# Four layers of cross-attention and feed-forward on one core: the first gated products fed from TensorE, setup reordered

## The chip, the core and the metric

One core of one Trainium2 chip. The metric is the device time of one execution in microseconds, from the kernel's runs; the profile is of one execution. All tensors are float32. In the names below, PE is TensorE, DVE is VectorE, ACT is ScalarE, POOL is GpSimd and SP is the queue that issues the DMAs.

## The reference, cut to what matters

Eight sequences (B=8) of 128 rows and 128 columns pass through four layers, each a cross-attention and a feed-forward block, each with a layer norm in front and a residual around it:

```python
x = x + L0_xattn(ctx, ctx, layernorm(x))
x = x + L0_ffn(layernorm(x))
x = x + L1_xattn(layernorm(x), ctx, ctx, masks)
x = x + L1_ffn(layernorm(x))
x = x + L2_xattn(layernorm(x), ctx, mask)
x = x + L2_ffn(layernorm(x))
x = x + L3_xattn(layernorm(x), ctx, ctx, bias)
x = x + L3_ffn(layernorm(x))
```

The block that matters most here is `L0_ffn`, an attention whose values and outputs are mixtures of experts, with 8 heads and 8 experts a head:

```python
gate_v, gate_o = sel_gate(x, sel_v_w), sel_gate(x, sel_o_w)   # two of eight experts, sigmoid, normalised, dense [S, 8, 8]
v = einsum('bshep,bshe->bhsp', einsum('bsd,hedp->bshep', x, v_w), gate_v)
att = softmax(einsum('bhqp,bhkp->bhqk', q, k) * SCALE)
ctx = einsum('bhqk,bhkp->bqhp', att, v)
out = einsum('bshep,hepd->bsd', ctx[..., None, :] * gate_o[..., None], o_w)
```

## The kernel before

The eight sequences are taken as four pairs of two (a lane each). The work is cut into four streams. *Early* (`early_pair`, letter p in the order table) does layer 0's attention of a pair and everything of `L0_ffn` up to the gates and the transposed probabilities. *Front* (`front_pair`, letter f) does the expert products of `L0_ffn`. *Back* (`back_lane`, letters 0 and 1 for the two lanes) does layers 1 to 3 of a pair. `late_setup`, at the head of stream 0, folds and centres weights once. Each engine has its own list of steps of each stream, and `ORDER`, a table written out by hand for each engine, says which stream takes its next step (`weave`, L353). Every engine works through that list in order; semaphores connect them.

A pair's expert products are 32 tiles of eight products: 16 for the values (head n // 2, lane n % 2), four mixing steps, and 16 for the outputs. A tile needs the gated rows, `gated` (128 x 1024): the transposed activations times the gate of each of eight experts, where the gate of a row stands in every partition. To bring it there, VectorE transposes the gates in blocks of 32 (`turn_gates`, L1542), SP stores them to a DRAM tensor in four pieces so that rows come out as columns (L404), and loads eight rows back, broadcast to all partitions, 512 KB a tile (`spread_gates`, L382); VectorE then multiplies in place (`gated_tile`, L1576, an instruction recorded at L1433). There are six slots for `gated` and four for the experts' weights, 512 KB each and one for two tiles; a load waits until the products that used its slot are done. All DMAs go through SP, in the order of its table.

The core of the front on TensorE (`expert_products`):

```python
pe.wait_ge(f_gated_ready, n + 1)
for e in range(E):
    ins = mm(to, gated[n % G_SLOTS][:, S * e:S * e + S],
             weights[j % W_SLOTS][:, D * e:D * e + D], first and e == 0, last and e == E - 1)
```

A float32 product shows in the trace as two matmul instructions (passes), a transposition as one; a tile is thus 16 passes. PSUM has eight banks: `e_bank` for expert products, `p_bank` for the early stream, and three for each lane. For pair 0, lane 0's early units use `e_bank` (`unit_bank`, L350), so pair 0's first expert product waits until the early stream is through.

`late_setup` on TensorE (L633) makes the folded q-k products, the total for layer 1's ternary weights, two value folds, the bias and mean of `proj`, and then the centred weights of layers 1 to 3, in six banks; ScalarE copies each result out (L1074), VectorE computes thresholds, the ternary weights, the length sums and scalings (L1617). The back's lanes wait on all engines for the last of these (`CENTRED`), GpSimd's masks of lane 0 and 1 among them (`masks`, L1336). `first_loads` (L416) issues all weights at the start. ScalarE's Gelu in layer 1's feed-forward (L1177) and in layer 2's (L1216) needs another activation table than the exponentials; a table load stands in the trace wherever the function changes. After the last front, TensorE does SPARE = 24 groups of three transpositions of the identity in its order's gaps (L627).

Of the kernel before, what the change touches and what calls it, by code (L numbers as in the profile page):

```python
# [11 lines left out]
E = 8  # L12
# [9 lines left out]
SPARE = 24  # L22
TILES = 4 * H0F
# [21 lines left out]
    "PE": "pppppp000p0pppp0ppp0000ppppppfpffpfpffpffpffpffpffffpfpfpfpfpfffffpffffpffpfffffp00p01p10pffff010pf0"  # L45
          "ff000fp00f00pffp0f0p10ff1ff00pf001f0110fp0f0p0110100000100101f10p0f11p0f11f10001f01f1p1ff1f11p1111f1"
          "0p0110f10f10011p010ff1pff0p001p10p10pfff1f0101ffff1p10ffffp1f11p0fpf1f01p010f10fp10f010f11pf00p1f111"
          "1f10p11f110011f101010ff0101pf0p01f11p0f00011000p00010110f011p1001f1101fp0f0010ff1001p10100f11f100110"
          "f0fp11f1f10p101ff00ff00f010000pf0010ff00f010110f01100101f1110f1100f101f1011001ff10ff101010110100010f"
          "ff100011f1f10111010f10f01101f11f1010fff11101010101ff1fffffff1f1ffff101011110010101011001101001001101"  # L50
          "00f0ffff10110011101000000000101101000011101000100101011f111100101101fffff",
    "Activation": "pppppp0p0pp000ppp00pppppppppp000pfppfpfpfpfpfpfp0fppppppp000p01p01fp00000000ppf010p001p0f0111f0f001f"
                  "0p11fp000110p000011f10p1111p01100011001pp11111p0010p00001100011pp011p00p1ppp11110f01111pf000fp1111p0"
                  "0p1f1000f11f01f000pf1p1110011p11111110111000p111p0010pp10p00001101p0011p0p11000000111000p10111001000"
                  "0p111111f011p10100f000p0001010000f01p110001110011f00111f110f10f11f1010011101101010000000110101001110"
                  "1111000001111111110101011111011100101110001101010011100101000110011100100000100001010000011001011011"
                  "011111011100011",
    "DVE": "pppppp0p0pppppp00pppppppppppp0ppffpppfppffffpffpffppffffppppfffffppfpppfpffpppffppfppfpffpppffppffff"
           "ffffp01f0000000f0fffp11f10fpf0001ffp1p11fp1000f00f000f100ppp0000p10000p0p1111ffffff1001101f01ff0p011"
           "ppp10111110pp1p11ffppff0ppp1100000010p11101f0ff0ffff1pppp0fffff000p1ff11ff0000p111111fff1p011pp11p11"  # L60
           "1110ff01pfppppff110fff01101010ff110f01p1f100p0ppp111100f0010000p000pp11p1111fpppp000000f01f01111ppp1"
           "1ppf10ffff0f00000001f01110111110ff11ff1ff0000ff0000111fff0011f100011000011000111ff001110000f1f11f000"
           "010ffff0011100000111111f10ffff111101111000f00f0010011111111f10ff101011111101001000101111001010010101"
           "010110001111000000110000011100000001011111011000000001111111110101",
    "Pool": "ppppfff1110000110100000p00011p11000000011110111110010001111fff1001p00000111p111000111110101011001001"
            "100000111f1ff010001100001000111010111010100011010000111111101f01ff0101111100001111000101010000010011"
            "1011",
    "SP": "ppffpffffffffpffffffffffffffffffffpffffpfffffffffffffpffffffffffffff0f1ffpffpfffffffffffffffffffpfff"
          "ffffffff10ffffff1fpffff0ffffpfffffffffffff0ffff1f1fffff0fffffff0011fff",
}  # L70


def width(members):
    return sum(n for _, n in members)


def build(nc, x_in, ctx_in, q_mask, k_mask, pair_mask, packs, experts, gates_of, out):
    with ExitStack() as stack:
# [3 lines left out]
        def sem(name):  # L82
            return stack.enter_context(nc.semaphore(name))
# [1911 lines left out]
```

## Time and profile before

| what | value |
|---|---|
| median of three runs | 682.85 us (681.27 to 683.88) |
| the profiled execution's own time | 681.64 us |
| its span, first to last instruction | 680.0 us |
| TensorE busy | 631.2 us (93%), 5480 passes |
| VectorE busy | 515.6 us (76%) |
| ScalarE busy | 372.9 us (55%) |
| GpSimd busy | 209.4 us (31%) |
| moved by DMA | 113.98 MB, mean 168 GB/s |

The span is what the trace covers; the own time is what the runs measure, 1.64 us more. Matmuls are pipelined and their ends are modelled, so a busy TensorE is not one at its peak: the number of passes in a stretch says more. Durations in the rows are microseconds unless marked ns; L464 is the helper that records every product, L980 ScalarE's copies, L1429 to L1436 VectorE's helpers, so tiles tell more than lines. Idle time in brackets names what ended it.

### The profile page before, as it was taken

Reading aid. Unit: us, or ns where it says so; the run is one execution under the profiler, and the core shown is the slowest. Engines: PE = TensorE matmul, PEld = TensorE weight load, DVE = VectorE, ACT = ScalarE, POOL = GpSimd, SP = SyncE. Lnnn points to the kernel's source line nnn. Section 1 sums busy time; section 2 is a strip of 40 time slices with the busy share of each in tenths; the row PEclk is TensorE's granted clock in tenths of the full one; section 3 lists DMA queues with packets and bytes.
Section 4 is the critical chain, followed back from the end, with each engine's and each line's share of the span. In section 5 each row is a group of like instructions: output and inputs, shape, how many; then the busy total and the mean of one; then the engine's idle time right before and its main releaser. Section 6 shows DMA issues by size and latency. Waiting matters only on the chain.

```text
span 680.0 us, 14643 instructions
## 1 busy us (share of the span) xinstructions
PE 631.2 (93%) x5480; PEld 576.7 (85%) x5480; DVE 515.6 (76%) x1419; ACT 372.9 (55%) x1257; POOL 209.4 (31%) x252
## 2 busy tenths in 40 slices
PE   5979999989999999998999999989999989899888
PEld 4868999868889999998789998977889989668877
DVE  1987678657678888895797889888368967657766
ACT  2361231346563667434845867356775563787594
POOL 0000000773440233231612625054243350642150
PEclk9899999979999999999999999999999999999999
DMA  8969969857704372987245316575416520000000
GB/s 321 402 237 298 364 239 334 303 180 271 239 1 159 99 265 72 340 267 269 77 155 192 109 32 191 189 239 173 156 28 229 171 79 1 6 1 1 1 2 12
DMA packets 37654, 113.98 MB, mean 168 GB/s; under 512 B 9040, under 2 KB 11728, under 8 KB 37072
## 3 DMA queue, kind: packets, MB, share of 16 engines
q1 hardware_dynamic: 37584, 113.06, 48.8%
q8 instruction: 43, 0.70, 0.4%
q14 instruction: 27, 0.22, 0.1%
HBM read 111.99 MB, written 1.05 MB: 166 GB/s over the span
## 4 chain that ended last, share of the span: by engine, by line
PE 53%; DVE 24%; ACT 11%; DMA 5%; POOL 5%; issue 3%; SPq 1%; DVEq 0%; POOLq 0%; ACTq 0%
PE bank L464 23%; PE e_bank L464 20%; DVE gated L1433 7%; ACT wide_b L1125 6%; PE p_bank L464 4%; DMA gated<-gates_of 4%; DVE wide_b L1436 2%; DVE max_neg L1721 2%; PE bank L721 2%; ACT wide_a L980 1%; DVE x L1436 1%; DVE f_route L1433 1%; DVE f_xn L1430 1%; ACT L1177 1%; PE bank L710 1%
## 5 line engine op out<-in xcount | busy, mean ns | idle before, releaser
L464 PE MATMUL e_bank<-weights,gated 128*128 128x128 f32 x2048 | 244.4, 277 | 2.4 <-DVE gated L1433 1.3
L464 PEld LDWEIGHTS e_bank<-weights,gated 128*128 128x128 f32 x2048 | 236.7, 193 | 6.3 <-issue 2.5
L1125 ACT ACTIVATE wide_b<-wide_b,max_neg 128x120 f32<-128x120 f32 x272 | 103.6, 388 | 22.7 <-DVE max_neg L1721 17.7
L1331 POOL TENSOR_TENSOR wide_b<-wide_b,row_inv 128x480 f32<-128x480 f32 x64 | 69.2, 1087 | 111.4 <-DVE row_inv L1726 111.1
L1433 DVE TENSOR_TENSOR gated<-gated,f_xnT 128x1024 f32<-128x1024 f32 x64 | 82.3, 1313 | 10.6 <-DMA gated<-gates_of 9.8
L1323 POOL TENSOR_TENSOR rstd<-var_eps,w_const 128x1 f32<-128x1 f32 (+1 forms) x48 | 35.2, 736 | 168.7 <-DVE var_eps L1429 168.5
L1433 DVE TENSOR_TENSOR gated<-gated,f_v 128x1024 f32<-128x1024 f32 x64 | 76.9, 1232 | 10.6 <-ACT f_v L980 5.5
L980 ACT ACTIVATE wide_a<-bank 120x512 f32<-120x512 f32 (+5 forms) x111 | 57.7, 540 | 43.9 <-PE bank L721 21.8
L1125 ACT ACTIVATION_READ_ACCUMULATOR wide_b<-wide_b,max_neg 128x1 f32 x272 | 52.6, 193 | 0.0
L1721 DVE TENSOR_REDUCE max_neg<-wide_b 128x4 f32<-128x480 f32 x64 | 41.8, 653 | 2.2
L721 PE MATMUL bank<-w_const,wide_b 128*120 128x128 f32 x256 | 37.4, 275 | 6.0 <-POOL wide_b L1331 5.9
L980 ACT ACTIVATE f_v<-e_bank 128x512 f32<-128x512 f32 x32 | 19.2, 600 | 37.6 <-PE e_bank L464 37.3
L721 PEld LDWEIGHTS bank<-w_const,wide_b 128*120 128x120 f32 x256 | 28.6, 138 | 12.1 <-issue 9.2
L1216 ACT ACTIVATE wide_a<-bank,w_L2f 128x128 f32<-128x128 f32 x128 | 34.8, 400 | 4.7 <-PE bank L464 4.7
L980 ACT ACTIVATE xnT<-bank 128x128 f32<-128x128 f32 x48 | 13.4, 282 | 37.8 <-PE bank L710 37.7
L464 PE MATMUL bank<-xnT,w_L2f 128*128 128x128 f32 x256 | 31.9, 278 | 0.0
L464 PE MATMUL bank<-w_L2f,wide_a 128*128 128x128 f32 x256 | 31.8, 275 | 0.0
L464 PEld LDWEIGHTS bank<-w_L2f,wide_a 128*128 128x128 f32 x256 | 30.2, 192 | 0.6 <-issue 0.5
L464 PEld LDWEIGHTS bank<-xnT,w_L2f 128*128 128x128 f32 x256 | 30.0, 192 | 0.1
L980 ACT ACTIVATE wide_b<-bank 128x480 f32<-128x480 f32 (+2 forms) x40 | 20.7, 523 | 15.1 <-PE bank L464 15.1
L1726 DVE RECIPROCAL row_inv<-row_sum 128x4 f32<-128x4 f32 x64 | 10.5, 170 | 23.8 <-ACT wide_b L1125 23.6
L1030 ACT ACTIVATE f_b<-p_bank,f_max_neg 128x128 f32<-128x128 f32 x56 | 19.7, 366 | 13.7 <-DVE f_max_neg L1495 13.7
(264 smaller groups left out, 1221.6 us busy)
## 6 DMA issues: line engine op xcount, KB each, us to landing
gated<-gates_of SPq DMA_DIRECT2D x128, 512.0 KB, 5.7
weights<-in_experts SPq DMA_DIRECT2D x64, 512.0 KB, 6.2
w_L2f<-in_L2f SPq DMA_DIRECT2D x1, 2124.0 KB, 14.6
w_L3x<-in_L3x SPq DMA_DIRECT2D x1, 2108.0 KB, 19.5
w_L3f<-in_L3f SPq DMA_DIRECT2D x1, 1128.0 KB, 21.6
wide_b<-in_raw0f SPq DMA_DIRECT2D x1, 1024.0 KB, 7.8
w_L1f<-in_L1f SPq DMA_DIRECT2D x1, 516.0 KB, 10.6
x_next<-in_x SPq DMA_DIRECT2D x4, 128.0 KB, 5.1
```

Source lines behind the costliest of these rows:

```text
L464: return nc.tensor.matmul(o, lhsT, rhs, start=first, stop=last)
L721: last = nc.tensor.transpose(bank[lane][(1, 2, 0, 1)[i]][0:K, 128 * c:128 * c + 128], wide_b[lane][:, K * h:K * h + K], ident)
L980: return nc.scalar.activation(o, i, ACT.Identity, bias=bias, scale=scale)
L1030: last = nc.scalar.activation(f_b[lane][:, 128 * h:128 * h + 128], unit_bank(pair, lane)[:, 128 * c:128 * c + 128], ACT.Exp, bias=f_max_ne ...
L1125: last = nc.scalar.activation(p, p, ACT.Exp, bias=max_neg[lane][:, h:h + 1], accum_out=row_sum[lane][:, h:h + 1])
L1216: last = nc.scalar.activation(wide_a[lane][:, at:at + 128], bank[lane][(1, 0, 2, 1)[i]][:, 128 * c:128 * c + 128], ACT.Gelu, bias=part["L2 ...
L1323: nc.gpsimd.tensor_tensor(rstd[lane][:, cols], var_eps[lane][:, cols], part["const", "minus_half"][:, 0:cols.stop - cols.start], ALU.pow)\
L1331: nc.gpsimd.tensor_tensor(p3, p3, row_inv[lane][:, 4 * i:4 * i + 4].unsqueeze(2).broadcast_to([128, 4, K]), ALU.mult).then_inc(probs_norme ...
L1433: return nc.vector.tensor_tensor(o, a, c, op)
L1436: return nc.vector.scalar_tensor_tensor(o, a, scalar, c, op0, op1)
L1721: nc.vector.tensor_reduce(max_neg[lane][:, 4 * i:4 * i + 4], s3, AX.X, ALU.max, negate=True)\
L1726: nc.vector.reciprocal(row_inv[lane][:, 4 * i:4 * i + 4], row_sum[lane][:, 4 * i:4 * i + 4])\
```

## The change

Eight edits go together:

1. **Spread on TensorE.** The first TURNED = 8 tiles of pair 0 don't go through DRAM. TensorE transposes a column of `f_gate`, repeated 128 times, so that the gate stands in all partitions: four such transpositions fill a bank with four experts' gates (`turn_first_gates`), in the three banks of lane 1 by turns. VectorE multiplies from PSUM in halves of 128 x 512 into one of two buffers in `wide_b[0]`. The spread loads of these tiles go.
2. **Early units.** For pair 0, lane 0's early units use `bank[0][2]` instead of `e_bank`, and the first expert product no longer waits for the transposed probabilities.
3. **Setup in two banks.** From the value folds on, setup's products use `bank[0][0]` and `bank[0][1]` by turns (the second value fold `bank[1][2]`), each waiting for ScalarE's copy of the bank's content before. The last fold waits for `ROUTED_IN`.
4. **Loads.** The packs L2x, L3x and L3f go ahead of the experts' first weights, which get a semaphore for each slot; layer 1's context goes behind the lengths.
5. **Zero products.** VectorE clears a tile `idle`; TensorE multiplies it with itself 7 times at the start, and 3, 3, 1, 5, 1 and 4 times behind the steps of pair 0's first attention, into `e_bank`, which no one reads.
6. **Early Gelu loads.** Right after the transposed x of layer 1's feed-forward is copied, ScalarE does a Gelu of one column of ones into `gelu_once`, eight times in all.
7. **memset.** Clearing `gate` goes from `late_setup` to the start.
8. **Order.** `ORDER` is new for all five engines. At the start, VectorE's length sums and the scaling of `proj` come behind pair 0's first gates, TensorE's mean of `proj` and all centring behind the first expert products, the last folds and GpSimd's masks of lane 0 ahead of the end of pair 0's front. SP issues the store of the second gates ahead of tile 8's load.

```diff
+TURNED = 8
...
+        first_gated = [wide_b[0][:, 1024 * i:1024 * i + 1024] for i in range(2)]
+        first_spread = [bank[1][i] for i in range(3)]
...
         def unit_bank(pair, lane):
-            return e_bank if pair == 0 and lane == 0 else p_bank
+            return bank[0][2] if pair == 0 and lane == 0 else p_bank
...
-                    if n % 16 == 0:
+                    if n % 16 == 0 or n == TURNED:
                         sp.wait_ge(f_gates_stored[t], 64 * (pair + 1))
-                    if n >= G_SLOTS:
+                    if n >= TURNED + G_SLOTS:
                         sp.wait_ge(f_expert_psum, n - G_SLOTS + 1)
...
-                        spread_gates(TILES * pair + n)
-                        yield
+                        if TILES * pair + n >= TURNED:
+                            spread_gates(TILES * pair + n)
+                            yield
...
                     sp.dma_start(part["L0f"][:, :], packs["L0f"]).then_inc(loaded["L0f"], 16)
-                    for j in range(W_SLOTS):
-                        sp.dma_start(weights[j][:, :], experts[:, E * D * j:E * D * (j + 1)]).then_inc(first_experts, 16)
                     sp.dma_start(part["L1f"][:, :], packs["L1f"]).then_inc(loaded["L1f"], 16)
                     sp.dma_start(raw2x[:, 0:2 * D], packs["raw2x"]).then_inc(loaded["raw2x"], 16)
-                    sp.dma_start(ctx_back[:, :], ctx_in[:, 0:2 * K]).then_inc(first_ctx_back, 16)
+                    for pack in ("L2x", "L3x", "L3f"):
+                        sp.dma_start(part[pack][:, :], packs[pack]).then_inc(loaded[pack], 16)
+                    for j in range(W_SLOTS):
+                        load_weights(j)
...
+                def keep_busy(count):
+
+                    for _ in range(count):
+                        mm(e_bank[:, 0:128], idle[:, :], idle[:, :])
...
                     last.then_inc(fold_products, 1)
+                    keep_busy(3)
                     yield
...
-                        pe.wait_ge(f_gated_ready, n + 1)
+                            pe.wait_ge(f_weights_loaded[j % W_SLOTS], 16 * (j // W_SLOTS + 1))
+                        if n < TURNED:
+                            pe.wait_ge(f_halves_gated, 2 * n + 2)
+                            rows = first_gated[n % 2]
+                        else:
+                            pe.wait_ge(f_gated_ready, n - TURNED + 1)
+                            rows = gated[n % G_SLOTS]
...
+                    def turn_first_gates(i):
+
+                        n, half = i // 2, i % 2
+                        if i == 0:
+                            pe.wait_ge(f_first_gates, 1)
+                        if i == 2:
+                            pe.wait_ge(setup_taken, VALUES_TAKEN)
+                        if i >= 3:
+                            pe.wait_ge(f_halves_gated, i - 2)
+                        for c in range(4):
+                            at = 64 * (n % 2) + E * (n // 2) + 4 * half + c
+                            last = nc.tensor.transpose(first_spread[i % 3][:, 128 * c:128 * c + 128],
+                                                       f_gate[:, at:at + 1].broadcast_to([128, 128]), ident)
+                        last.then_inc(f_spread_psum, 1)
...
-                            else:
-                                pe.wait_ge(p_pT_ready.sem, p_pT_ready.upto(L0F, 4, pair))
...
                     centre = part["const", "centre"]
-                    pe.wait_ge(qk_taken, 2)
-                    mm(bank[0][2][:, :], centre, part["L1f", "fc"]).then_inc(centre_products, 1)
+                    pe.wait_ge(setup_taken, BIAS_TAKEN)
+                    mm(bank[0][0][:, :], centre, part["L1f", "fc"]).then_inc(centre_products, 1)
                     pe.wait_ge(loaded["L2x"], 16)
-                    mm(bank[1][2][:, 0:D], part["L2x", "wq"], centre).then_inc(centre_products, 1)
+                    pe.wait_ge(setup_taken, PROJ_MEAN)
+                    mm(bank[0][1][:, 0:D], part["L2x", "wq"], centre).then_inc(centre_products, 1)
...
                     take_xT(lane, L1F)
+                    nc.scalar.activation(gelu_once[:, 2 * pair + lane:2 * pair + lane + 1], part["const", "ones"][:, 0:1], ACT.Gelu)
                     yield
...
+                        if t == 0 and pair == 1:
+                            dve.wait_ge(f_spread_psum, 2 * TURNED)
...
+                        for half in range(2):
+                            dve.wait_ge(f_spread_psum, 2 * n + half + 1)
+                            tt(first_gated[n % 2][:, 512 * half:512 * half + 512].rearrange("p (e s) -> p e s", s=S),
+                               first_spread[(2 * n + half) % 3][:, :].rearrange("p (e s) -> p e s", s=S),
+                               rows.unsqueeze(1).broadcast_to([128, 4, S]), ALU.mult).then_inc(f_halves_gated, 1)
+                            yield
```

The beginnings of the old and the new order on TensorE (the new one has steps for the zero products and the spread):

```diff
-    "PE": "pppppp000p0pppp0ppp0000ppppppfpffpfpffpffpffpffpffffpfpfpfpfpfffffpffffpffpfffffp00p01p10pffff010pf0"
+    "PE": "ppppppp000ppp0pppp0pfffffpffpffffffffpp00fpffpf0pfpffpffp0pffffp0pffffpfpfpfpfpfffff0pffpffpffffpffffpf"
```

## Rows read from the trace of the kernel before

**Rows 1.** the page, the chain that ended last, shares of the span by engine
```profile
PE 53%; DVE 24%; ACT 11%; DMA 5%; POOL 5%; issue 3%; SPq 1%; DVEq 0%; POOLq 0%; ACTq 0%
```

**Rows 2.** windows by stage: stretch, length, busy time (instructions) per engine, clock, DMA share, GB/s
```profile
0.00:45.36 45.36, 32.23 (x170) 26.34 (x171) 28.28 (x84) 18.20 (x64) 2.32 (x7) 0.96 0.86 321
45.36:121.30 75.94, 73.36 (x641) 72.20 (x642) 56.01 (x108) 18.25 (x62) 2.10 (x3) 1.00 0.88 306
121.30:147.30 26.00, 22.13 (x144) 18.11 (x143) 17.05 (x33) 10.60 (x38) 22.75 (x28) 0.87 0.73 263
147.30:269.30 122.00, 119.00 (x1082) 111.81 (x1081) 98.07 (x268) 74.24 (x253) 38.36 (x48) 1.00 0.46 156
...
419.70:576.70 157.00, 146.90 (x1343) 136.07 (x1342) 120.51 (x342) 87.65 (x276) 55.39 (x62) 1.00 0.46 149
576.70:680.00 103.30, 91.32 (x787) 76.02 (x785) 69.40 (x253) 72.40 (x249) 35.68 (x43) 1.00 0.01 4
```

**Rows 3.** the chain in order of time: start, length, what
```profile
10.97 2.07 PE p_bank L464 x8
...
18.76 1.13 DVE abs_sum L1621 x2
...
28.65 2.12 DVE lens L1644 x2
...
34.17 0.32 DVE f_gateT L1545
...
37.76 5.76 DMA gated<-gates_of
...
80.75 0.89 PE p_bank L464 x8
```

**Rows 4.** windows of the start, and of the setup products
```profile
0.00:10.00 10.00, 4.25 (x17) 3.71 (x18) 1.71 (x8) 2.58 (x5) 1.43 (x6) 1.00 0.78 259
10.00:20.00 10.00, 7.73 (x32) 6.49 (x31) 3.59 (x14) 1.56 (x6) 0.89 (x2) 1.00 1.04 408
31.75:37.16 5.41, 5.41 (x25) 3.04 (x23) 4.95 (x17) 3.10 (x15) 0.00 (x0) 1.00 0.36 130
```

**Rows 5.** TensorE's transpositions by form: durations of one, min/median/max in ns
```profile
L564 PEld LDWEIGHTS p_bank<-w_const,f_b x56: 137/141/144, 42.7 to 470.5; 128*128 128x128 f32 x56
L564 PE MATMUL p_bank<-w_const,f_b x56: 272/273/328, 42.7 to 470.6; 128*128 128x128 f32 x56
```

**Rows 6.** VectorE by line and form: count, busy us, mean ns
```profile
L1433 DVE TENSOR_TENSOR gated<-gated,f_xnT 128x1024 f32<-128x1024 f32 x64 | 82.3, 1313 | 10.6 <-DMA gated<-gates_of 9.8 <-DVE route L1433 0.3
...
L1433 DVE TENSOR_TENSOR wide_a<-wide_a,bank 128x512 f32<-128x512 f32 x8 | 5.5, 686 | 4.1 <-PE bank L958 3.9 <-ACT wide_a L1255 0.2
```

**Rows 7.** the chain between 121 and 137 us
```profile
121.24 0.44 PE p_bank L564 x4
121.68 1.96 PE bank L464 x10
...
124.59 0.19 POOL pair_lens L1338
...
136.26 0.52 POOL mask L1352
```

**Rows 8.** TensorE's timeline from 121 us, with the idle time before in brackets
```profile
121.08 0.60 PE L564 MATMUL p_bank<-w_const,f_b 128*128 128x128 f32 x4
...
138.00 2.03 PE L464 MATMUL bank<-wide_a,small 32*128 32x480 f32 x12 [2.60 <-POOL wide_a L1360]
140.84 1.94 PE L464 MATMUL bank<-wide_a,small 128*128 128x480 f32 x2 [0.81 <-POOL wide_a L1366]
```

**Rows 9.** window behind those waits; the clock is the third column from the end
```profile
142.00:144.00 2.00, 2.00 (x8) 1.53 (x8) 1.93 (x5) 2.00 (x13) 2.00 (x2) 0.50 0.06 25
```

**Rows 10.** the Gelu of layer 1's feed-forward: ns min/median/max, first to last start
```profile
L1177 ACT ACTIVATE wide_b<-bank,rstd x8: 681/687/687, 167.8 to 611.6; 128x512 f32<-128x512 f32 x8
L1177 ACT ACT_TABLE_LOAD  x5: 1283/1283/1283, 166.5 to 603.6; - x5
```

More of the change, by code:

```diff
@@ L52 @@
[L52 to L64, printed above, removed]
@@ L484, in early_pair @@
                     last.then_inc(p_kv_psum.sem, 1)
+                    if pair == 0:
+                        keep_busy(3)
                     yield
@@ L496, in early_pair @@
                     turn_xn(L0X)
+                    if pair == 0:
+                        keep_busy(1)
                     yield
@@ L1095, in late_setup @@
                         act.wait_ge(centre_products, Q3 - 1 + half)
-                        copy(part["L3x", "wq"][:, 512 * half:512 * half + 512], bank[half][1][:, :]).then_inc(centred, 1)
+                        copy(part["L3x", "wq"][:, 512 * half:512 * half + 512], bank[0][half][:, :]).then_inc(centred, 1)
                         yield
@@ L1101, in late_setup @@
                     act.wait_ge(centre_products, GATE_FC1)
-                    copy(part["L3f", "gate"], bank[1][0][:, 0:E], scale=-1.0)
-                    copy(centred_fc1[0:64, :], bank[1][0][0:64, 128:256]).then_inc(centred, 1)
+                    copy(part["L3f", "gate"], bank[0][1][:, 0:E], scale=-1.0)
+                    copy(centred_fc1[0:64, :], bank[0][1][0:64, 128:256]).then_inc(centred, 1)
                     yield
@@ L1106, in late_setup @@
                         act.wait_ge(centre_products, folded)
-                        copy(part["L3f", name], bank[half][1][:, :]).then_inc(centred, 1)
+                        copy(part["L3f", name], bank[0][half][:, :]).then_inc(centred, 1)
                         yield
                     act.wait_ge(centre_products, Q2)
-                    copy(part["L2x", "wq"], bank[1][2][:, 0:D]).then_inc(centred, 1)
+                    copy(part["L2x", "wq"], bank[0][0][:, 0:D]).then_inc(centred, 1)
                     yield
@@ L1452, in early_pair @@
                     x_now = f_x[pair % 2]
+                    if pair == 0:
+                        nc.vector.memset(idle[:, :], 0.0).then_inc(idle_filled, 1)
+                        nc.vector.memset(gate[:, :], 0.0)
+                        yield
                     dve.wait_ge(x_loaded, 16 * (pair + 1))
```

134 lines of the change are left out of this document (91 added, 43 removed).

## The prediction

> **What bounds the kernel now.** I read the page's chain first: TensorE carries 53% of what ended last, VectorE 24%, DMA 5% [rows 1]. To see where TensorE is full, I then read the span by stage, cut at the first gated product (45.36 us), the end of pair 0's front (121.30), the point where pair 0's back runs freely (147.30), pair 1's front end (269.30) and pair 3's (576.70) [rows 2]. The reader should see passes per us: 8.4 from 45.36 on and 8.9 from 147.30 on, but 3.7 in the first 45.36 us and 5.5 between 121.30 and 147.30. At full rate eight passes of 128 columns take 0.89 us (at 80.75) [rows 3], 0.111 us each. So from 45 us on TensorE sets the pace nearly everywhere, and the kernel has two holes, one at each end of pair 0's front. The last 103.3 us are the two lanes of the last pair; no front work is left there, and the change leaves them nearly as they are.
>
> The first hole [rows 3]: at 10.97 eight passes take 2.07 us, the slow rate; VectorE does setup (2.12 us of length sums, among others) in front of the gates; the gates are turned at 34.17, stored to DRAM, spread from there (5.76 us for the piece on the chain) and multiplied from 43.5. The second hole [rows 7, 8]: the masks of both lanes run on GpSimd from 124.59 to 136.8, because they wait for the last centred weight; lane 0's blocks follow, and TensorE waits 2.60 and 0.81 us for them.
>
> **The change, part by part**, against the profiled execution's own 681.64 us (span 680.0 and 1.64 around it).
>
> *Zero products.* Eight passes of the first scores take 2.07 us, against 0.89 later [rows 3]. The clock column says 1.00 there, yet the same pitch stands where it says 0.50 [rows 4, 9], so I take it for the lower level, 1.2 GHz. If the zero products lift it, scores gain 1.2 us, the two small products behind them 0.9; the key products gain nothing, since the transposition behind them waits for the normalised x, which waits for the constants and not for TensorE. Sum 2.1 us. Bounds: if the zeros themselves run slowly, they overrun their gaps and cost up to 2 us; at most 3 us is gained. I take 2, since the engine is fed from before the first load lands.
>
> *Setup behind the gates.* Length sums (2.12) and the scaling of proj (0.7) go behind the gates; the ternary part stays ahead, in time in which VectorE waits for logits. abs_sum moves before x, and costs up to 0.8 us where fc lands late. The gates come at 27.8 instead of 34.2: 2.0 from the clock, 2.8 from the two moved steps, and 1.6 since abs_sum (1.13, and some 1 us of steps beside it) stood between x and its normalisation and now stands ahead, less its 0.8 there.
>
> *Spread on TensorE.* Store, spread load and wait (34.5 to 43.5) go for the first 8 tiles. In their place stand gate transposition and one maximum (1.0 us) and two halves of 128x512 read from PSUM, 0.69 us each by the row of the same shape and operands [rows 6]. First product at 27.8 + 1.0 + 1.4 = 30.2, against 45.36: 15.2 us sooner. VectorE pays 16 x 0.69 = 11.0 for 8 x 1.31 = 10.5, so 0.5 more; it stays ahead of TensorE, for its last half comes at about 54 and TensorE reaches that tile at about 57. TensorE pays 64 transpositions. Four in a row take 0.60 us, one 0.27, its load 0.14 beside it [rows 5, 8]: 0.11 each, 7.1 us; 16 lie before the first product and cost nothing, 48 behind it cost 5.3. No row has a stationary operand that is one column repeated; bounds 0.11 (in a row) and 0.41 (load and pass one after the other), and I take 0.11, since these too stand four in a row with a load apiece. The Trainium skill, TensorE: Matmul & The Clock Gate, Part 4: PE-mode transpose, gives 390 ns for one alone and about 275 ns in one kernel, and says that transpositions don't keep the clock up. By 275 ns the 48 would cost 13.2 us instead of 5.3, and the sum would be +1.2. The row of one alone (0.27) agrees, the row of four in a row does not.
>
> *What TensorE must now do behind the first product.* Of what ran before 45.36, these come later: centring and the mean of proj, 5.4 us [rows 4]; two score fills, 1.8; four transposed fills, 1.8. From behind 121.3 the last folds come forward, 1.96 and 0.44 [rows 7]. With the 5.3 that is 16.7 us. The stretch to the end of pair 0's front had 75.9 us with 2.6 idle [rows 2]; I halve the idle, since eight spread loads (4 MB) are gone. The two banks add waits for ScalarE's copies; the one with its copy right ahead (the second centring behind the mean of proj) is worth some 0.6 us, within that half. It becomes 75.9 + 16.7 - 1.3 = 91.3, and 30.2 + 91.3 = 121.5 against 121.3: the 15 us are used up, term **+0.2**. TensorE has what work there is, so what is done sooner saves only its idle time.
>
> *Loads.* Weights are issued behind 4.0 MB more, so after 6.3 MB; 2.59 MB land by 10 us and 6.67 by 20 [rows 4], by the packs' widths, so they are there by about 21 to 25, before 30.2. SP stands in its order at the store of the second gates until about 48, and tile 8's load is queued behind it: between the turned gates and the spread load's issue lay 3.3 us, its landing took 5.8 [rows 3], so it is there at about 57. TensorE needs it at about 61. Cost nothing, 4 us of cover; each us more on VectorE ahead of the second gates eats one. The eight spread loads that go leave SP sooner free for the next x, which waits for nothing new.
>
> *The second hole.* The folds gone from it give back 1.96 + 0.44 = 2.4. The masks are now begun under pair 0's last products. The waits of 2.60 and 0.81 [rows 8] go, and so does the low clock that followed (granted 0.50 [rows 9]): 1.94 us for the last key product, about 1.0 too long; eight passes 0.8 and a tile 1.2 too long. Together 6.4. But TensorE's order now has only 2.1 us of work between the front's end and lane 0's scores, and the way there (sum, statistics, root on GpSimd, xn, transposition, copy, blocks) takes about 5.3: a new wait of 3.2. Net 3.2, and with the folds term **-5.6**. Bounds: 0 if the lower clock comes again, -8.8 if the wait is filled.
>
> *Gelu table.* Five loads of 1.283 us come right before the Gelu [rows 10]; the early one-column activation moves them under the wait for the product, and the new order has two switches fewer. Where TensorE is full this is worth nothing; in the last 103 us it is. One load: term **-1.3**, bounds 0 and -6.4. The eight added activations are some 0.2 us each on an engine that is 55% busy. The Trainium skill, ScalarE: Activation LUTs, What ACT_TABLE_LOAD costs, adds a drain of 1.38 us to each switch, which would make this term -2.7; in this trace the first load starts at 166.5 and its activation at 167.8, as the load ends [rows 10], so the row stands.
>
> *The rest of the order table* is re-dealt in all pairs. Passes are the same; idle later on, 3.0 us by the busy column up to 269.30 and 10.1 in the last front's stretch [rows 2], may shrink or grow. The gates of pair 1 wait for the last spread transposition, done half a pair earlier: nothing. Taken at nothing, bounds +7 and -7.
>
> Sum: +0.2 - 5.6 - 1.3 = -6.7, so 674.9 where the profiled execution had 681.64. The median of the runs, 682.85, lies 1.2 above that, so I forecast **676**.
>
> **Rivals.** (a) *More than forecast*: the new wait is covered (-3.2), no idle is left in front 0 (-1.3), and all five table loads pay (-5.1): 666. For: TensorE's queue has gated tiles ready for a filler. Against: its order is fixed, and the scores stand before pair 1's first tile. (b) *Given back on GpSimd*: lane 1's masks now stand behind lane 0's first blocks and ahead of lane 0's third block and its normalisation, and the next layer norm's root behind them. Both lanes' masks took 12 us beside a busy VectorE [rows 7]; lane 1's half, 6, would hold lane 0's probabilities: 682. Against: six tiles, over 10 us of TensorE, lie between. (c) *Transpositions dear*: the repeated column loads badly or each pass runs alone. At 0.27 us the 64 cost 10.2 us more where all count: 686; with load and pass one after the other, 0.41, they cost 19.2 more: 695, slower. Its place is TensorE between 28 and 58 us; it decides from about 0.21 us each, where the gain is gone, and is slower by over 0.5% from about 0.27. Against: the row of four. The rule on transpositions cited above would make this case. (d) *The zeros do not lift the clock*: 2 to 4 us lost of idle saved at the start: 679.
>
> **How the numbers follow.** Forecast 0.40, (a) 0.20, (b) 0.18, (c) 0.12, (d) 0.10. A measurement of this kernel can tell about 0.5%, 3.4 us, from no change: faster is below 679.4, slower above 686.3. Faster: nearly all of the forecast, (a), and half of (d): 0.62. Same: (b) but for a little, a third of (c), the other half of (d), the forecast's edge: 0.26. Slower: the rest of (c), and what the re-dealt order may lose on top of (b): 0.12. Range 664 to 687: from (a) to the lower end of (c), with the upper end of (c) and an order worse by over 7 us left out.
>
> **What would show it.** Right: first gated product near 30 us; eight early score passes near 0.9 us; four spread transpositions in about 0.6; pair 0's front ending within 3 us of 121; no wait of TensorE for the blocks of 2.6 us behind a mask, and pair 1's front ending 5 to 7 us sooner than 269.3; a table load of Gelu that ends before its product does. Wrong: a front 0 that ends by 116 (then work was cheaper than counted) or after 125 (spread dear, or tile 8 late); equal lead at 269 and none at 577 (the order gave it back).

## The result, and the profile after

The changed kernel takes **658.40 us**, the median of four runs (655.86 to 659.37), against 683.37 of the kernel before in the same session: a ratio of 0.9628, with a 95% interval of 0.9599 to 0.9658, so 25 us or 3.7% less. The forecast was 676, with a range of 664 to 687: the sign was right, the size was not, and the time lies below the range. The profiled execution has a span of 657.6 us and 659.37 in all, the slowest of the four.

The chain of the changed kernel, shares of the span by engine; it answers to [rows 1]:

```profile
PE 87%; ACT 5%; DVE 4%; DMA 3%; issue 1%; POOL 1%; SPq 0%; DVEq 0%; ACTq 0%
```

VectorE had 24% of it, and has 4%. The windows by stage, with the columns of [rows 2], cut at the first product (33.38), the end of pair 0's front (123.0), the point where the back runs freely (150), and the ends of pair 1's and pair 3's fronts (260.6, 550.2):

```profile
0.00:33.38 33.38, 28.34 (x181) 25.95 (x181) 18.14 (x61) 10.12 (x31) 2.32 (x7) 0.90 0.95 369
33.38:123.00 89.62, 88.89 (x759) 85.83 (x760) 66.77 (x141) 28.07 (x101) 9.41 (x11) 1.00 0.68 235
123.00:150.00 27.00, 23.94 (x195) 21.07 (x194) 21.77 (x42) 12.35 (x48) 17.95 (x22) 1.00 0.93 326
150.00:260.60 110.60, 110.60 (x1020) 104.39 (x1019) 91.63 (x267) 72.86 (x253) 35.06 (x47) 1.00 0.46 156
260.60:550.20 289.60, 289.21 (x2653) 271.06 (x2652) 240.83 (x669) 174.30 (x582) 103.43 (x124) 1.00 0.52 173
550.20:657.60 107.40, 95.49 (x795) 78.55 (x793) 69.88 (x254) 73.13 (x251) 35.78 (x43) 0.97 0.01 4
```

From 150 to 550.2 TensorE's busy column misses 0.4 us of 400.2. In the kernel before, 3.0 us were missing from 147.3 to 269.3 and 10.1 in the last front alone [rows 2].

The table below holds the end of each pair's front, which is the start of VectorE's addition of the bank to `f_x` (the same four instructions in every trace), the span, and TensorE's idle time in the stage that ends there (its length less the time in which a pass ran). All kernels of this study stand in it, in the order in which they come.

```
kernel           front 0  front 1  front 2  front 3   span    idle by stage               table loads
before            121.3    269.3    419.7    576.7   680.0   15.7  6.9  4.2 10.1 12.0     23
changed           123.0    260.6    393.1    550.2   657.6    5.8  3.1  0.1  0.3 11.9     21
new_tail          120.3    267.1    401.1    560.1   669.7   13.7  4.3  1.0  1.8 13.6     21
old_tail          119.8    270.5    423.1    578.7   682.1    5.6 11.9  5.6  7.6 12.1     27
old_from260       122.4    260.5    414.1    569.7   672.8    5.0  3.5  6.1  7.6 11.8     25
no_gelu           120.6    261.0    394.6    553.5   663.0    6.5  4.1  0.9  1.8 13.3     21
gelu_in_before    120.8    271.5    424.7    580.3   683.4   15.3  9.2  6.4  7.6 11.8     27
no_zeros          121.2    260.5    392.9    550.1   657.0   10.2  3.2  0.0  0.3 12.5     21
no_spread         129.0    268.0    400.6    557.7   665.0   17.9  2.7  0.2  0.3 11.7     21
early_ctx         121.6    258.9    391.4    548.5   655.2    5.5  2.4  0.0  0.3 12.5     21
turned4_ctx       118.1    255.2    387.4    544.6   651.9    6.6  2.1  0.0  0.3 11.7     21
turned2_ctx       124.4    261.5    393.8    551.0   659.4   12.0  2.1  0.0  0.3 12.5     21
```

Read the first two lines against each other. Pair 0's front ends no sooner, as forecast. Then 10.4 us are gained in pair 1's stage (148.0 to 137.6) and 17.9 in pair 2's (150.4 to 132.5), none in pair 3's; the tail gives 4.1 back. Pair 2's 17.9 are not all gain: 1,323 passes of TensorE start in that stage before and 1,191 after, and 1,341 and 1,460 in pair 3's. Work of the lanes has moved one stage on. What is gained for good in the two is the idle time, 4.2 and 10.1 us against 0.1 and 0.3.

### The profile page after: what moved, and what is told of

It is laid out like the page before. It is cut to its first block, busy times and chain, and to the rows that moved or that the text cites. A ratio compares the mean times of both kernels' runs of the same rounds, so it can differ in the third digit from the quotient of the medians.

```text
span 657.6 us, 14887 instructions
## 1 busy us (share of the span) xinstructions
PE 636.5 (97%) x5592; PEld 586.9 (89%) x5592; DVE 509.0 (77%) x1428; ACT 370.8 (56%) x1263; POOL 204.0 (31%) x252
## 4 chain that ended last, share of the span: by engine, by line
PE 87%; ACT 5%; DVE 4%; DMA 3%; issue 1%; POOL 1%; SPq 0%; DVEq 0%; ACTq 0%
PE bank L476 36%; PE e_bank L476 36%; PE p_bank L476 5%; PE bank L780 4%; ACT wide_b L1184 2%; ACT wide_a L1039 1%; PE bank L625 1%; DMA gated<-gates_of 1%; PE bank L769 1%; DMA ctx_front<-in_ctx 1%; DMA w_const<-in_const 1%; PE p_bank L592 1%; PE e_bank L683 1%; DVE x L1496 1%; PE bank L1017 1%
## 5 line engine op out<-in xcount | busy, mean ns | idle before, releaser
L476 PE MATMUL e_bank<-weights,gated 128*128 128x128 f32 x1920 | 226.3, 275 | 0.8 <-DVE gated L1493 0.7
L476 PEld LDWEIGHTS e_bank<-weights,gated 128*128 128x128 f32 x1920 | 220.2, 192 | 3.3 <-issue 2.2
L1391 POOL TENSOR_TENSOR wide_b<-wide_b,row_inv 128x480 f32<-128x480 f32 x64 | 65.9, 1039 | 121.6 <-DVE row_inv L1808 121.6
L1039 ACT ACTIVATE wide_a<-bank 120x512 f32<-120x512 f32 (+5 forms) x111 | 57.9, 542 | 43.2 <-PE bank L476 20.1
L1383 POOL TENSOR_TENSOR rstd<-var_eps,w_const 128x1 f32<-128x1 f32 (+1 forms) x48 | 33.1, 690 | 133.5 <-DVE var_eps L1489 133.3
L1493 DVE TENSOR_TENSOR gated<-gated,f_xnT 128x1024 f32<-128x1024 f32 x56 | 68.0, 1244 | 2.9 <-DMA gated<-gates_of 2.2
L1337 POOL TENSOR_TENSOR f_rstd<-f_var_eps,w_const 128x2 f32<-128x2 f32 x8 | 9.0, 1125 | 65.3 <-DVE f_var_eps L1489 57.9
```

Source lines behind the costliest of these rows:

```text
L476: return nc.tensor.matmul(o, lhsT, rhs, start=first, stop=last)
L1039: return nc.scalar.activation(o, i, ACT.Identity, bias=bias, scale=scale)
L1337: return nc.gpsimd.tensor_tensor(to[:, :], rows[:, :], part["const", "minus_half"][:, 0:2], ALU.pow)
L1383: nc.gpsimd.tensor_tensor(rstd[lane][:, cols], var_eps[lane][:, cols], part["const", "minus_half"][:, 0:cols.stop - cols.start], ALU.pow)\
L1391: nc.gpsimd.tensor_tensor(p3, p3, row_inv[lane][:, 4 * i:4 * i + 4].unsqueeze(2).broadcast_to([128, 4, K]), ALU.mult).then_inc(probs_norme ...
L1493: return nc.vector.tensor_tensor(o, a, c, op)
```

## The experiments

Three theories. **Theory 1**: what came beyond the forecast lies in the re-dealt order table. **Theory 2**: it lies in the edits (the early Gelu loads, the moved waits), whatever the order. **Theory 3**: it is a lead that the lanes win behind pair 0's front and then keep, whatever the order.

### The order alone, and the edits alone

Each of three kernels takes one code and joins two orders. Each string of the order table is kept up to a point in time of that code's own trace; behind it come all steps that are left, in the relative order of the other kernel. GpSimd's string shows the edit; the other four engines are cut at the same time in the same way.

**new_tail**, the kernel before with the changed order from 121.3 us on:

```diff
-    "Pool": "ppppfff1110000110100000p00011p11000000011110111110010001111fff1001p00000111p111000111110101011001001"
+    "Pool": "pppp000f001111p000001f100f00110p110101110000111100110011011ff100001p0f0011111010p1011101101010010011"
...
```

> The kernel before with its order table up to 121.3 us (the end of pair 0's front in its own trace), and from there on the relative order of the changed kernel. Nothing of the code differs from the kernel before. Theory 1: pair 0's front ends at 121.3, then 137.6 + 132.5 + 157.1 + 107.4 us, some 6 more for the masks that begin no sooner, so 656 to 664. Theory 2 and theory 3: within 1% of the kernel before, 677 to 688.

Measured: 671.80 us against 683.17, a ratio of 0.9854 (0.9817 to 0.9892). The order alone gains 11.4 us by the medians, without one edit of the code. That is between the theories' figures, and tells that neither holds all of it. Its trace has 14.1 us less idle time of TensorE in the stages of pairs 1 to 3 (table), but is only 10.3 us shorter: its granted clock from 123 to 150 us is 0.75, against 0.87 behind pair 0's front in the kernel before [rows 2], and the last stage has 1.6 us more idle time.

**old_tail**, the changed kernel with the order of before from 123.0 us on:

```diff
-    "Pool": "pppp000f001111p000001f100f00110p110101110000111100110011011ff100001p0f0011111010p1011101101010010011"
+    "Pool": "pppp000fff1110110100000p00011p11000000011110111110010001111fff1001p00000111p111000111110101011001001"
...
```

> The changed kernel with its order table up to 123.0 us (the end of pair 0's front in its own trace), and from there on the relative order of the kernel before on all five engines. Nothing of the code differs from the changed kernel. Theory 1 (the gain beyond the forecast lies in the re-dealt order of pairs 1 to 3): the stages of the kernel before come back behind a front that ends at 123, 137.6 to 148 + 150.4 + 157.0 + 103.3 us, so 672 to 682. Theory 2 (the edits, the early Gelu loads and moved waits, take TensorE's idle time out of the later pairs, whatever the order): 656 to 662. Theory 3 (the lead of the front part carries it: the lanes begin sooner and stay in step): 656 to 664, with a pair 1 front that ends by 262.

Measured: 684.6 us, a ratio of 1.0026 (1.0009 to 1.0043). All 25 us are gone, with every edit in place: theories 2 and 3 fall as explanations of the whole. The figure goes beyond theory 1, too, and the seam has a part in that: TensorE waits 5.9 us for gated tiles right behind 123 us, 4.3 of them at once, and VectorE's product for that tile had waited 5.0 us for a spread load. How much of the figure the seam makes is not shown.

**old_from260**, cut where TensorE is full:

```diff
-    "Pool": "pppp000f001111p000001f100f00110p110101110000111100110011011ff100001p0f0011111010p1011101101010010011"
+    "Pool": "pppp000f001111p000001f100f00110p110101110000111100110011011fff1001p00000111p111000111110101011001001"
...
```

> The changed kernel with its order table up to 260.6 us (the end of pair 1's front in its own trace), and from there on the relative order of the kernel before on all five engines. The seam now lies in a stretch where TensorE is full, not in the hole behind pair 0's front. Theory 1 (the order of pairs 2 and 3 takes out TensorE's waits there, 14.1 us in the kernel before from 269.3 to 576.7, 0.2 in the changed one): these waits come back, pair 2's and pair 3's fronts take some 150 and 157 us again and the tail 103, so 668 to 673. Theory 3 (the lanes' lead, once it is there at 260.6, carries on by itself): 656 to 661.

Measured: 672.84 us, a ratio of 0.9844 (0.9814 to 0.9873). Up to 260.5 us it takes the steps of the changed kernel; behind it pair 2's stage takes 153.6 us and pair 3's 155.6. So 14.4 us hang on the order behind 260.6 us, and a lead, once there, does not carry on by itself: theory 3 falls.

What TensorE waits for from pair 1's front end to pair 3's, by what released it: us in total, times, the longest. First the kernel before, 269.3 to 576.7, the six largest of ten rows:

```profile
PE bank L721 <- POOL wide_b L1331: 3.7, 3, 3.0
PE bank L802 <- ACT wide_b L1177: 2.1, 2, 1.3
PE bank L464 <- DVE wide_b L1436: 1.9, 1, 1.9
PE p_bank L492 <- DVE f_xn L1430: 1.6, 2, 1.2
PE p_bank L507 <- ACT f_b L996: 1.4, 1, 1.4
PE bank L464 <- ACT wide_b L980: 1.2, 2, 0.8
```

The changed kernel, 260.6 to 550.2, the only row:

```profile
PE bank L476 <- ACT wide_a L1039: 0.2, 1, 0.2
```

new_tail, 267.1 to 560.1, all rows:

```profile
PE bank L802 <- ACT wide_b L1177: 1.6, 2, 1.3
PE bank L464 <- ACT wide_b L980: 0.9, 1, 0.9
PE bank L464 <- ACT wide_a L980: 0.3, 1, 0.3
```

old_from260, 258 to 560, the first four of ten:

```profile
PE bank L780 <- POOL wide_b L1391: 4.2, 4, 3.0
PE bank L476 <- DVE wide_b L1496: 1.9, 1, 1.9
PE e_bank L476 <- DVE gated L1493: 1.9, 1, 1.9
PE bank L476 <- ACT wide_b L1039: 1.2, 2, 0.8
```

Before, the ten rows sum to 14.1 us. They are no single late step: GpSimd's scaled probabilities, ScalarE's Gelu, VectorE's blocks, each a little later than its place in TensorE's string. The new order alone leaves 2.8, most of it the Gelu (L1177), and the old order brings the same waits back, the 3.0 us for GpSimd among them. The steps of the code are the same under both orders; what the order changes is which other steps stand ahead of one that gives or needs a result. Whether the results now come sooner or TensorE asks for them later, and which of the moved entries does it, is not shown.

### The early Gelu loads

**no_gelu**, the changed kernel without them:

```diff
-                    nc.scalar.activation(gelu_once[:, 2 * pair + lane:2 * pair + lane + 1], part["const", "ones"][:, 0:1], ACT.Gelu)
+                    pass
```

> The changed kernel without the one-column Gelu activations; order table as changed. Theory 1, with the forecast's term: 1.3 us more, bounds 0 and 6.4, so 658 to 665. Theory 2: the table loads stand ahead of TensorE again in each pair, 10 us or more, 668 to 676.

Measured: 665.60 us, a ratio of 0.9745 (0.9721 to 0.9770), 7.2 us more than the changed kernel by the medians. The profiled spans differ by 5.4, but this execution had its first gated product 2.4 us sooner, before the edit has any part (30.95 against 33.38, see the next section). From the end of pair 0's front on it takes 7.8 us more, 542.4 against 534.6: 2.8, 1.1 and 1.8 in the stages of pairs 1 to 3 and 2.1 in the last. The table loads are as many, 21. TensorE's largest wait in this trace, over the whole span:

```profile
PE bank L861 <- ACT wide_b L1237: 3.6, 4, 1.3
```

and the Gelu's own line, durations in ns:

```profile
L1237 ACT ACTIVATE wide_b<-bank,rstd x8: 687/688/689, 157.8 to 591.0; 128x512 f32<-128x512 f32 x8
L1237 ACT ACT_TABLE_LOAD  x6: 1283/1283/1283, 156.5 to 581.8; - x6
```

Four times TensorE waits for the Gelu, the longest wait as long as one load. In the changed kernel the six loads stand at the one-column activation (L1233) and this wait is in no row. The other 4.2 us of the 7.8 are not one wait: that for `f_xn` is 2.1 us against 1.4, and the granted clock from 121 to 150 us is 0.94 against 1.00; whether that fall of the clock comes of the edit is not shown.

**gelu_in_before** puts the same activation into the kernel before, order as it was:

```diff
+        gelu_once = sb("gelu_once", [128, B])
...
                     take_xT(lane, L1F)
+                    nc.scalar.activation(gelu_once[:, 2 * pair + lane:2 * pair + lane + 1], part["const", "ones"][:, 0:1], ACT.Gelu)
```

> The kernel before with the one-column Gelu activations added, its order table unchanged. If the early loads pay by themselves (the forecast's term, one load of 1.283 us, or up to five): 677 to 682. If they pay only with an order that lets no Exp step come between the one-column activation and the Gelu proper (the changed order with the old one from 123 us on had 27 table loads against 23): no gain or a loss, 683 to 688, with 25 or more table loads.

Measured: 685.53 us, a ratio of 1.0038 (1.0021 to 1.0055): 0.4% slower. ScalarE's table loads by line in this trace, the three groups that grew or are new (L1126 had 8 before; L1175 is the one-column activation, L1179 the Gelu):

```profile
L1126 ACT ACT_TABLE_LOAD x10 | 12.8, 1283 | 0.2
L1175 ACT ACT_TABLE_LOAD x5 | 6.4, 1283 | 0.1
L1179 ACT ACT_TABLE_LOAD x2 | 2.6, 1283 | 0.0
```

Twice an Exp step stands between the early activation and the Gelu, fetches its own table and makes the Gelu fetch again: 27 loads against 23. The edit and the order are one change; half of it is a loss.

### The start

**no_zeros**:

```diff
                 def keep_busy(count):
 
-                    for _ in range(count):
+                    for _ in range(0):
                         mm(e_bank[:, 0:128], idle[:, :], idle[:, :])
```

> The changed kernel without the zero products (the order and all waits stay). Theory 1, with the forecast's terms: gates 2 us later, first gated product near 35.4 instead of 33.4, and the end of pair 0's front by up to 2 us later, 658 to 661. Theory 3: the lead is worth its full length, 660 to 661, or more where the lanes fall out of step. If the zero products hold the early work up: 656 to 658.

Measured: 660.49 us, a ratio of 0.9669 (0.9640 to 0.9697), 2.1 us more than the changed kernel; the two intervals overlap by 0.2%, so that figure is likely and not shown. TensorE's timeline of this kernel (start, length): the 16 passes that fold the query and key weights, and the first gated product:

```profile
16.53 3.28 PE L476 MATMUL bank<-wide_b 128*128 128x128 f32 x16
...
32.63 2.02 PE L476 MATMUL e_bank<-weights,wide_b 128*128 128x128 f32 x16
```

and of the changed kernel, with the first eight key products and the first 16 transpositions between them:

```profile
14.93 1.95 PE L476 MATMUL bank<-wide_b 128*128 128x128 f32 x16
...
20.20 2.05 PE L476 MATMUL bank<-f_xnT,qk 128*128 128x128 f32 x8 [0.70 <-ACT f_route L1039]
...
31.15 2.18 PE L625 MATMUL bank<-w_const,f_gate 128*128 128x128 f32 x16 [0.70 <-DVE f_gate L1493]
33.38 2.02 PE L476 MATMUL e_bank<-weights,wide_b 128*128 128x128 f32 x16
```

The 16 passes of the fold take 3.28 us without the zero products and 1.95 with them, so with them these passes do run at the upper level. At 20.20 the profiled execution of the changed kernel fell back: eight passes take 2.05 us, 1.13 in no_zeros. The window of that stretch has the granted clock at 0.51 (third column from the end), and 1.00 in no_gelu, whose first 30 us hold the same steps; changed kernel first:

```profile
20.00:27.00 7.00, 6.80 (x31) 6.38 (x32) 4.77 (x15) 1.97 (x6) 0.00 (x0) 0.51 1.03 403
```

```profile
20.00:27.00 7.00, 6.30 (x54) 5.94 (x54) 6.13 (x19) 3.50 (x10) 0.00 (x0) 1.00 1.02 404
```

In no_gelu the first product starts at 30.95, in the changed kernel's profiled execution at 33.38. Against 32.63 in no_zeros the zero products thus bring it 1.7 us forward where the clock holds, and nothing in the execution where it fell.

**no_spread**, no tile spread by transpositions; PE's and VectorE's strings lose the steps that go:

```diff
-TURNED = 8
+TURNED = 0
...
-    "SP": "ppppffffffffffffffffffpfffffffffffpffpfffffffffffffffffffffffffff0ppffffffffffff0f1fpfffffffffffffff"
+    "SP": "ppffpffffffpffffffffffffffffffpfffffffffffpffpfffffffffffffffffffffffffff0ppffffffffffff0f1fpfffffff"
...
-                    if pair == 0:
+                    if pair == 0 and TURNED:
                         for i in range(2):
                             turn_first_gates(i)
```

> The changed kernel with TURNED = 0: no tile is spread by transpositions, the first eight again by spread loads from DRAM; the 64 transpositions, their order entries and the 16 halves go, eight whole products and eight loads come in. Zero products, setup behind the gates, loads and the rest of the order stay. The forecast's step (the lead of the first product is used up, since TensorE has what work there is): the first product comes at 42 to 44 instead of 31 to 33, TensorE saves 5.3 us of transpositions behind it, and nothing else is there for it in between, so pair 0's front ends 4 to 6 us later and the kernel takes 662 to 664. If the lead is worth its full length: 668 or more. If it is worth nothing at all: 657 to 660.

Measured: 667.82 us, a ratio of 0.9784 (0.9758 to 0.9810), 9.4 us more than the changed kernel. TensorE's timeline, the first product of this kernel:

```profile
40.39 3.75 PE L476 MATMUL e_bank<-weights,gated 128*128 128x128 f32 x16 [11.80 <-DVE gated L1493]
```

It waits 11.80 us, and then runs at the lower clock (3.75 us for 16 passes, 2.02 in the changed kernel). In all TensorE idles 17.9 us up to the end of pair 0's front, against 5.8 (table). Pair 0's front ends 6.0 us later than in the changed kernel's trace, and all later fronts some 7.5: what is lost there stays lost to the end.

### What is left

**early_ctx** moves one load of SP:

```diff
-    "SP": "ppppffffffffffffffffffpfffffffffffpffpfffffffffffffffffffffffffff0ppffffffffffff0f1fpfffffffffffffff"
+    "SP": "ppppffffffffffffffffffppfffffffffffffpfffffffffffffffffffffffffff0ppffffffffffff0f1fpfffffffffffffff"
```

The reason is the one large wait of TensorE behind pair 0's front in the changed kernel:

```profile
130.30 0.48 PE L476 MATMUL p_bank<-ctx_front,l_fold 128*128 128x120 f32 x2 [1.85 <-DMA ctx_front<-in_ctx]
```

> The changed kernel with one entry of SP's order moved: the load of the third pair's x and context stands right behind the store of pair 1's first gates (97.6 us) instead of behind eleven spread loads (124.2 us). What it waits for was done by 60 us. The reading that TensorE's wait of 1.85 us at 130.3 is this load's landing alone: the wait goes, and with it what is left of the second hole, 1 to 2.5 us less, 656 to 657.5. If the wait is then taken over by the next late step (masks, blocks, the low clock): no change, 658 to 659.

Measured: 656.58 us, a ratio of 0.9610 (0.9590 to 0.9631). The wait is gone; part of it comes again one step later:

```profile
127.03 0.48 PE L476 MATMUL p_bank<-ctx_front,l_fold 128*128 128x120 f32 x2
...
129.24 2.02 PE L476 MATMUL e_bank<-weights,gated 128*128 128x128 f32 x16 [1.06 <-DVE gated L1493]
```

By the medians 1.8 us less than the changed kernel, but the intervals overlap, and the gain is not shown. Of the 2.4 us between the profiled spans, 1.3 are there at the first gated product (32.06 against 33.38), which comes before the moved load; in pair 1's stage, where the wait stood, it is 0.3 us (137.6 to 137.3).

**turned4_ctx** adds `TURNED = 4`, with the strings to match (four spread loads behind the first store on SP; eight transposition steps go from PE's string, and eight half products become four whole ones on VectorE):

```diff
-TURNED = 8
+TURNED = 4
...
-    "SP": "ppppffffffffffffffffffpfffffffffffpffpfffffffffffffffffffffffffff0ppffffffffffff0f1fpfffffffffffffff"
+    "SP": "ppffffpffpffffffffffffffffppfffffffffffffpfffffffffffffffffffffffffff0ppffffffffffff0f1fpfffffffffff"
...
```

> The kernel early_ctx with TURNED = 4: tiles 4 to 7 come by spread loads, issued behind the store of the first gates (33 us) and landed some 6 us later, by about 40; TensorE needs tile 4 at about 46. Saves 32 transpositions of 0.11 us on TensorE, 3.5 us, and on VectorE 8 halves against 4 whole products. If the lead of the front is work on TensorE alone: 3 to 3.5 us less than early_ctx, 652.5 to 654.5. If the loads come late or the lead is lost in the second hole: the same as early_ctx.

Measured: **653.66 us**, a ratio of 0.9563 (0.9536 to 0.9590), below the changed kernel's interval: this version is faster than either kernel. Pair 0's front ends at 118.1 against 121.6 in early_ctx. Of these 3.5 us, 0.45 are there at the first product already (31.61 against 32.06); 3.0 are left for 32 transpositions. At the end of the span the lead is 3.3.

**turned2_ctx** goes one step further, with strings to match (against the changed kernel):

```diff
-TURNED = 8
+TURNED = 2
...
```

> The kernel turned4_ctx with TURNED = 2: tiles 2 to 7 come by spread loads. Saves 16 more transpositions of 0.11 us, 1.8 us, and TensorE wants tile 2 at about 36 us, while the spread loads issued from 33 us on land some 6 us later. If the loads set the pace there, TensorE waits 3 us or more for tile 2 and its clock may fall: 654 to 658. If tile 2 is there in time: 651 to 653.

Measured: 658.16 us, a ratio of 0.9641 (0.9612 to 0.9671). Tile 2 is late, and the wait is paid twice, by the clock that follows (6.63 us for 32 passes, 3.74 at 38.79 in turned4_ctx):

```profile
40.99 6.63 PE L476 MATMUL e_bank<-weights,gated 128*128 128x128 f32 x32 [4.89 <-DVE gated L1493]
```

## Why the prediction was wrong in size

Two of the runs make a path from the kernel before to the changed one. The order from 121.3 us on, alone: 683.2 to 671.8, **-11.4**. Then all edits at the start, the loads and the new early order, without the Gelu: 671.8 to 665.6, **-6.2**. Then the early Gelu: 665.6 to 658.4, **-7.2**. The prediction had 0, +0.2 - 5.6 = -5.4, and -1.3. The runs do not cut where the forecast's terms end: the waits for GpSimd's blocks, which the forecast had in the second hole, go with the order here. On another path the parts would have other sizes (the Gelu edit is worth -7.2 behind the new order and +2.6 by the ratio ahead of it), but the sum of the three is what was measured.

**The order table: the step that failed.** "The rest of the order table is re-dealt in all pairs ... Taken at nothing, bounds +7 and -7." The order alone gave 11.4, outside its bounds. The waits of 2.60 and 0.81 us behind the masks are in that figure; but behind pair 1's front, where they have no part, new_tail's trace is still 8.1 us shorter than the one before (402.6 against 410.7), and in the changed kernel the order behind 260.6 us is worth 14.4. The rows held what was to be had: 3.0 and 10.1 us idle in [rows 2], 4.2 more in pair 2's stage (table above), 17 in all, of which the changed kernel has 0.4 left. The bound took less than half of that, with no row to say why. That sum was the lower bound to take.

**The Gelu table: right in kind, mis-sized.** "Where TensorE is full this is worth nothing; in the last 103 us it is." So the term took one load, -1.3, of bounds 0 and -6.4. Measured: 7.2 by the medians, 7.8 by the traces from the end of pair 0's front on (5.4 by whole spans), 5.7 of it in the stages of pairs 1 to 3. TensorE is full only as long as nothing in its string is late; its order is fixed, so a late Gelu stops it in the middle of a full stage as well: in no_gelu three of the four waits that sum to 3.6 us lie ahead of 553.5, in stages that are nearly full. That the activation pays only with an order made for it (gelu_in_before) was not in the prediction at all. The Trainium skill, ScalarE: Activation LUTs, What ACT_TABLE_LOAD costs, adds a drain of 1.38 us to a switch: the longest wait of 1.3 is a load of 1.283 without one, so the runs do not show it here.

**The second hole: inside its bounds, with other parts.** Forecast -5.6, bounds 0 and -8.8. Pair 1's stage goes from 148.0 in the kernel before to 146.8 in new_tail and 140.4 in no_gelu, -1.2 and -6.4. That is no clean measure of the term: some of the 3.0 us idle later in that stage, which the forecast had with the order, is in it, and the parts are not those forecast, so the agreement is partly luck. Pair 1's front ends 8.7 us sooner than 269.3 in the changed kernel, where 5 to 7 were forecast. The waits for the masks were to go with the earlier begin of the masks. They are gone in new_tail already (TensorE waits for nothing of GpSimd from 120.3 to 267.1 us), and its masks begin as far behind pair 0's front as before, 3.3 us (at 123.59, against 124.59); there the order removes them, with lane 0's blocks ahead of lane 1's masks:

```profile
123.59 0.19 POOL L1338 COPY pair_lens<-lens 128x2 f32<-128x2 f32 x1 [56.48 <-ACT w_L2x L980]
...
128.97 0.99 POOL L1366 TENSOR_TENSOR wide_a<-small,w_const 128x480 f32<-128x480 f32 x1
129.90 0.19 POOL L1338 COPY pair_lens<-lens 128x2 f32<-128x2 f32 x1
```

The folds and the low clock went with the start, as forecast: the granted clock from 123 to 150 is 0.75 in new_tail and 0.94 in no_gelu. And the new wait came, but not where it was put: 1.85 us for the load of `ctx_front` and not 3.2 for the blocks.

**The start: right.** Zero products 2 us: 1.7 at the first product where the clock holds, 2.1 by medians whose intervals overlap. Eight early score passes near 0.9 us: 1.17, against 2.07 [rows 3]. The gates at 27.8 and the first product at 30.2: 30.95 in no_gelu, and 33.38 where the clock fell at 20.1. Four spread transpositions in about 0.6 us: 64 by 273 ns each with a load of 133 to 139 ns beside it, eight in 1.04 us. Halves of 0.69: 0.68. Tile 8 in time: multiplied at 59, needed at 64.4. Pair 0's front within 3 us of 121: 123.0. "The 15 us are used up" holds for the package alone: with everything else in place the spread on TensorE is worth 9.4 us (no_spread): the setup stands behind the gates, and without an early first product TensorE has nothing to do ahead of it.

**The rivals.** (a), more than forecast, is what happened, and more so. It named the covered wait, the idle of front 0 and five table loads, the loads at 6.4 us, which came near the 7.2 measured; not the order. (b), lane 1's masks in the way of lane 0: TensorE has no wait for them. (c), transpositions dear: refuted. Eight of them stand 0.87 us ahead of the next product, 0.109 each, and 32 fewer give 3.0 to 3.5 us. Behind the first product, where 48 run, the granted clock is 1.00 (window 33.38 to 123.00). The Trainium skill, TensorE: Matmul & The Clock Gate, Part 4: PE-mode transpose, has 275 ns for one in a kernel; here that is what one lasts (273), and 0.109 is what each adds in a row. (d), the zeros do not lift the clock: refuted by the fold's passes, though the clock may fall again at 20 us. The lines for (c), of the changed kernel:

```profile
36.13 1.04 PE L625 MATMUL bank<-w_const,f_gate 128*128 128x128 f32 x8
37.00 1.06 PE L476 MATMUL p_bank<-f_xnT,f_b 128*128 128x128 f32 x8
```

## What to carry to other kernels

Where the order of every engine is written out, price a new order by the idle time of the bound engine in the stages that it re-deals, wait by wait, and not at nothing with a guessed margin: here the stages held 17 us, and the order took out most of it. A prefetch of a table, a weight or a mode is worth what its order lets it be: count the switches in the order that goes with it, and try the edit in the old order, where it may lose. And a replacement that costs the bound engine time (transpositions for loads) should stop at the tile that the cheap way can deliver in time: of eight, four and two, four was best here.

## What the runs showed of the hardware

Two waits of TensorE were paid a second time by its clock. Behind 11.80 us of idle time (no_spread) 16 passes take 3.75 us, with a granted clock of 0.50 from 40.39 to 44.20; behind 4.89 us (turned2_ctx) 32 take 6.63, with 0.55 over them. 0.5 is the lower of the two levels (1.2 GHz). At the upper (2.4 GHz) 16 take 1.95 and 32 take 3.74. Not every wait is: behind the 1.85 us at 130.3 in the changed kernel the clock stays at 1.00 (window 123 to 150).

And the same early steps meet the lower level in one execution and not in another. The granted clock from 20 to 27 us is 0.51 in the changed kernel's profile, 0.52 in old_from260's, 0.76 in early_ctx's and 1.00 in no_gelu's and old_tail's, whose first 30 us hold the same steps; their first products come at 33.38, 33.15, 32.06, 30.95 and 30.50 us. So a profile of a single execution can be nearly 3 us off at this place, whichever kernel it is, and two traces are better compared from the first product on.
